# One scratch tensor for queries and keys instead of four, and another order of ScalarE, VectorE and GpSimd work, in the projection stage of a two-layer recurrent and attention kernel

## The chip, the cores and the metric

The kernel runs on one core of one Trainium2 chip. The metric is the device time of one execution in microseconds (us). A core has a tensor engine (PE, with weight loads shown as PEld), a vector engine (DVE), a scalar engine (ACT), GpSimd (POOL), and SyncE (SP), which here only issues DMA transfers. Sixteen DMA engines move the data of all transfers.

## The reference

Four sequences of 2048 tokens with 256 channels go through two layers. Each layer computes `x = x + s(xn) * silu(g(xn))` with `xn = layernorm(x)`.

```python
# layer 0: s is a WKV recurrence over time, g is a two-matrix feed-forward net
# layer 1, the part around the change:
c_q = x @ W_DQ;   Qc = c_q @ W_UQ (16 heads x 16);  Qr = rope(c_q @ W_QR) (16 heads x 8)
c_kv = x @ W_DKV; Kc = c_kv @ W_UK (16 heads x 16); Kr = rope(x @ W_KR) (8, the same for every head)
V = c_kv @ W_UV (16 heads x 16)
Q, K = concat(Qc, Qr), concat(Kc, Kr)          # 24 per head
w = softmax(where(causal, clip(Q @ K.T, -80, 80), -inf) / sqrt(24));  s = (w @ V) @ W_O
r = sigmoid(xr @ W_r.T); k = square(relu(xk @ W_k.T)); g = r * (k @ W_v.T)
# xr = mu_r * x + (1 - mu_r) * x_prev, xk the same with mu_k; x_prev is x one token earlier
```

## The kernel before, in words

The program has four stages, one after the other, each a block that all engines leave together: layer 0, the projections of layer 1 (`layer1_projections`), attention, and the output. The change is in the second stage and in what it hands to the third.

**The projection stage** goes over 16 chunks of 512 tokens (4 sequences of 4 chunks). Every engine runs its own written-out program, in order, and semaphores tie them together. Where precision matters a number is kept as two float16 halves: ACT writes the high half (`..._high`), DVE or POOL subtracts it and writes the low half (`..._low`), and PE multiplies the halves. `n` is the chunk, and work for the chunks `n + 1` and `n + 2` is threaded into the body of chunk `n`:

- **PE**: latents (`lat`), gate keys (`k_mm`), shared rotary keys (`kr_mm`), content queries (`qc_mm`), rotary queries (`qr_mm`), transposes of chunk `n + 1` (L1403, into `ps_t`, which the rotary keys also use, so they wait for DVE's two reads at L1356, `kr_parts`), then the gate receptance `r_mm` with the content keys `kc_mm` in its middle, the values, and the last gate product `kv_mm` (L1472).
- **ACT**: relu of the gate keys (L1216), `qc` high (L1219), then `xn_of(n + 1)`: `xn` high (L1162), one edge column (L1171) and four operations that write `prev`, the scaled earlier token (L1176). `kc` high (L1223) stands between the second and the third of these. Then `kr` high, the sigmoid, the values, `xk` high (L1185), `qr` high (L1240), `xr` high (L1191), the latents, `normalise(n + 2)` (four operations, L1156) and the gate's sigmoid (L1247).
- **DVE**: low halves of the latents, the two rotary key products (L1356), `qc` low, the two rotary query products, the statistics of chunk `n + 2` (`layernorm`, L1259), `kc` low (L1368), `xn` low (L1271, waits for all of `prev`), `mix` (L1280: two operations for `x_k`, two for `x_r`), `xk` low (L1285), `aggregate(n + 2)` (L1266), `qr` low (L1378), and the gate product (L1383).
- **POOL**: the rotary sums, the square, `kr` low, `xr` low (L1096), `rstd_of(n + 2)` (L1087 to L1092, four small operations whose result `normalise` waits for), and the gate (L1126).
- **SP**: the stores of the chunk, each after the semaphore of its last writer: `qc`, `kr`, `kc`, `qr`, `v` (counted in `stored`, `STORES = 5` of them per chunk) and the gate, and a load of `x` for four chunks later (none in the last four chunks). Buffers alternate between two slots. ACT waits on `stored` before it writes `qc` of a chunk two later. After the stores of chunk 12 SP issues the 20 loads of the first attention group (`load_group`: 16 for queries and keys, 4 for values). SP leaves the block only when the last `stored` count is complete, so the third stage starts then.

The scratch tensors lie in DRAM: `qc_d` and `kc_d` hold `[batch, half, 256 channels, 2048 tokens]` in float16, `qr_d` the 128 rotary query rows, `kr_d` the 8 rotary key rows. A store of `qc` is one transfer of 128 partitions with four runs of 1 KB each (512 KB). A store of `kr` is one of 8 partitions (16 KB). In attention a head has 32 partitions of its own, 24 of them used: per head and for queries and keys each, one load brings 16 content partitions (2 halves of 4 KB runs, 128 KB) and another 8 rotary partitions (64 KB).

**The attention stage** goes over 16 groups of four heads. It loads the operands of the next group while it works on this one, one transfer of SP per step.

Of the kernel before, what the change touches and what calls it, by code (L numbers as in the profile page):

```python
# [770 lines left out]
def scratch(nc):  # L771

    def dram(name, shape, dt=F32):
        return nc.dram_tensor(name, shape, dt, kind="Internal").ap()

    return {
        "x1": dram("x1_d", [TOKENS, DIM]),
        "qc": dram("qc_d", [BATCH, 2, DIM, SEQ], F16),
        "qr": dram("qr_d", [BATCH, 2, HEADS * D_R, SEQ], F16),
        "kc": dram("kc_d", [BATCH, 2, DIM, SEQ], F16),  # L780
        "kr": dram("kr_d", [BATCH, 2, D_R, SEQ], F16),
        "v": dram("v_d", [BATCH, GROUPS, P, KEYT, GH * VW]),
        "gate": dram("gate_d", [TOKENS, DIM]),
        "attn": dram("attn_d", [DIM, TOKENS]),
    }
# [65 lines left out]
STORES = 5  # L851


def layer1_projections(nc, a, d, ident, rows_out, early, scales, first):
# [6 lines left out]
    with ExitStack() as ctx:  # L861
# [130 lines left out]
        gate_v3 = d["gate"].rearrange("(n j p) c -> n p j c", j=TPC, p=P)  # L992
        LEFT, RIGHT = slice(0, 2 * LATENT), slice(2 * LATENT, 4 * LATENT)
# [30 lines left out]
        with nc.Block() as block:  # L1024
            @block.sync
            def _(sp):
# [9 lines left out]
                def store(b, c):  # L1036
# [3 lines left out]
                    sp.dma_start(d["qc"][b, :, :, t].rearrange("h (m p) t -> p (h m) t", p=P),  # L1040
                                 qc[:, s].rearrange("p h m t -> p (h m) t")).then_inc(stored[s], 16)
                    sp.wait_ge(kr_low, n + 1 + 1)
                    sp.dma_start(d["kr"][b, :, :, t].rearrange("h p t -> p h t"), kr[:, s]).then_inc(stored[s], 16)
                    sp.wait_ge(kc_low, n + 1)
                    sp.dma_start(d["kc"][b, :, :, t].rearrange("h (m p) t -> p (h m) t", p=P),
                                 kc[:, s].rearrange("p h m t -> p (h m) t")).then_inc(stored[s], 16)
                    sp.wait_ge(qr_low, n + 1)
                    sp.dma_start(d["qr"][b, :, :, t].rearrange("h p t -> p h t"), qr[:, s]).then_inc(stored[s], 16)
# [24 lines left out]
            def _(pool):  # L1073
# [32 lines left out]
                def body(b, c, left):  # L1106
# [24 lines left out]
            def _(act):  # L1131
# [27 lines left out]
                def xn_of(n, c, between=None):  # L1159
# [14 lines left out]
                    for i in (1, 0):  # L1174
# [3 lines left out]
                        if i and between:  # L1178
                            between()

                def xk_high_of(n, first=False):
# [4 lines left out]

                def xr_high_of(n, first=False):
# [13 lines left out]
                xk_high_of(0, first=True)  # L1201
                xr_high_of(0, first=True)
# [10 lines left out]
                def body(b, c, left):  # L1213
# [6 lines left out]

                    def keys_high():
                        act.wait_ge(kc_mm, n + 1)
                        nc.scalar.activation(kc[:, s, 0], ps_c[:], ACT.Copy, scale=k_factor).then_inc(kc_high, 1)  # L1223
# [28 lines left out]
            def _(dve):  # L1252
# [15 lines left out]
                def xn_low_of(n):  # L1268

                    dve.wait_ge(prev_done, PREVS * (n + 1))  # L1270
# [3 lines left out]
                def mix(n, c, first=False):  # L1274
# [3 lines left out]
                    for i, t in ((1, x_k), (0, x_r)):  # L1278
                        for k in range(KT):
# [731 lines left out]
```

## Time and profile before

| | |
|---|---|
| time, median of 3 runs | 2110.49 us (2109.88 to 2111.5) |
| the profiled execution | 2109.88 us |
| its span, first to last instruction | 2107.9 us |
| layer 0 | 0 to about 690 us |
| projections of layer 1 | about 690 to 1028.7 us |
| attention | 1028.7 to about 2040 us |
| output | about 2040 to 2107.9 us |
| mean granted TensorE clock | 0.987 of full speed |

Times in the profile are microseconds from the first instruction. A row of the timeline gives start, duration, engine, line, operation, what is written from what is read, and in brackets how long the engine was idle before it and what released it. The stages are from the timeline. One page row gives the load over the whole span: PE busy 93%, ACT 77%, DVE 76%, POOL 27%.

### The profile page before, as it was taken

Reading aid. Unit: us, or ns where it says so; the run is one execution under the profiler, and the core shown is the slowest. Engines: PE = TensorE matmul, PEld = TensorE weight load, DVE = VectorE, ACT = ScalarE, POOL = GpSimd, SP = SyncE. Lnnn points to the kernel's source line nnn. Section 1 sums busy time; section 2 is a strip of 40 time slices with the busy share of each in tenths; the row PEclk is TensorE's granted clock in tenths of the full one; section 3 lists DMA queues with packets and bytes.
Section 4 is the critical chain, followed back from the end, with each engine's and each line's share of the span. In section 5 each row is a group of like instructions: output and inputs, shape, how many; then the busy total and the mean of one; then the engine's idle time right before and its main releaser. Section 6 shows DMA issues by size and latency. Waiting matters only on the chain. (4 is left out here: it accounts for less than half of the span.)

```text
span 2107.9 us, 54312 instructions
## 1 busy us (share of the span) xinstructions
PE 1970.0 (93%) x23334; PEld 998.0 (47%) x23334; DVE 1608.8 (76%) x2223; ACT 1628.8 (77%) x1945; POOL 576.9 (27%) x416
## 2 busy tenths in 40 slices
PE   5999999999999589999899999999999999999986
PEld 2655665565565255555433444333443333343335
DVE  7867766766764777877688888888888888888877
ACT  5545644544554677787799999999999999999972
POOL 1643554454455365666200000000000000000008
PEclk9999999999999799999999999999999999999999
DMA  3000010010011255556522222222221222221229
GB/s 104 21 21 21 21 41 21 21 41 21 21 55 37 99 180 168 189 174 136 194 66 73 70 68 59 67 70 68 72 72 55 68 69 52 61 61 45 67 86 322
DMA packets 130222, 166.29 MB, mean 79 GB/s; under 512 B 13632, under 2 KB 101696, under 8 KB 129728
## 3 DMA queue, kind: packets, MB, share of 16 engines
q1 hardware_dynamic: 127952, 160.59, 25.8%
q8 instruction: 185, 3.03, 0.6%
q10 hardware_dynamic: 2032, 2.24, 0.3%
q14 instruction: 53, 0.43, 0.1%
HBM read 91.21 MB, written 71.57 MB: 77 GB/s over the span
## 5 line engine op out<-in xcount | busy, mean ns | idle before, releaser
L1683 ACT ACTIVATE c_probs<-c_ps_b 128x1536 f32<-128x1536 f32 x544 | 857.4, 1576 | 0.0
L1795 PE MATMUL c_ps_o<-c_probs,c_v 128*32 128x256 f32 (+3 forms) x6656 | 582.5, 453 | 3.8 <-DVE c_probs L1715 0.8
L1715 DVE TENSOR_SCALAR c_probs<-c_probs 128x2048 f32<-128x2048 f32 (+2 forms) x415 | 434.1, 1056 | 69.8 <-ACT c_probs L1683 67.9
L1775 PE MATMUL c_ps_a<-c_qk 24*128 24x256 f16 (+2 forms) x2688 | 444.5, 291 | 21.9 <-ACT c_probs L1682 16.6
L1775 PE MATMUL c_ps_b<-c_qk 24*128 24x256 f16 (+2 forms) x8064 | 453.4, 294 | 0.0
L1682 ACT ACTIVATE c_probs<-c_ps_a 128x512 f32<-128x512 f32 x544 | 388.7, 715 | 3.4 <-PE c_ps_b L1775 1.8
L1775 PEld LDWEIGHTS c_ps_a<-c_qk 24*128 24x128 f16 x2688 | 206.1, 92 | 369.7 <-ACT c_probs L1683 188.3
L1942 POOL TENSOR_TENSOR d_prod<-d_prod,d_x 128x1024 f32<-128x1024 f32 x8 | 26.2, 3290 | 1025.5 <-DVE d_prod L1930 1025.5
L1795 PEld LDWEIGHTS c_ps_o<-c_probs,c_v 128*32 128x32 f32 x6656 | 161.7, 108 | 245.8 <-issue 126.6
L258 POOL TENSOR_TENSOR a_hidh<-a_hid,a_hidh 128x512 f16<-128x512 f32 x128 | 170.2, 1348 | 233.6 <-ACT a_hidh L356 229.8
L1775 PEld LDWEIGHTS c_ps_b<-c_qk 24*128 24x128 f16 x8064 | 212.3, 93 | 0.8 <-issue 0.2
L1720 DVE TENSOR_SCALAR c_probs<-c_probs 128x1536 f32<-128x1536 f32 (+2 forms) x208 | 164.6, 798 | 53.0 <-ACT c_probs L1683 50.9
L667 PE MATMUL a_ps<-a_xnh,a_w 128*128 128x512 f16 x768 | 172.0, 379 | 12.0 <-ACT a_hid L351 12.0
L667 PE MATMUL a_ps<-a_w,a_hidh 128*128 128x256 f16 x1536 | 170.3, 273 | 0.0
L1724 DVE SCALAR_TENSOR_TENSOR c_probs<-c_probs,c_caps 128x512 f32<-128x512 f32 x256 | 169.7, 684 | 0.0
L667 PEld LDWEIGHTS a_ps<-a_w,a_hidh 128*128 128x128 f16 x1536 | 150.2, 98 | 17.7 <-POOL a_hidh L258 0.2
L667 PEld LDWEIGHTS a_ps<-a_xnh,a_w 128*128 128x128 f16 x768 | 73.1, 97 | 105.0 <-ACT a_hid L351 19.9
L367 ACT ACTIVATE a_gp<-a_gp 128x1024 f32<-128x1024 f32 x16 | 16.9, 1058 | 122.3 <-DVE a_gp L531 122.3
L351 ACT ACTIVATE a_hid<-a_ps,a_b 128x512 f32<-128x512 f32 x128 | 86.1, 686 | 31.8 <-PE a_ps L667 25.7
L346 ACT ACTIVATE a_en<-a_en 128x1024 f32<-128x1024 f32 x16 | 17.0, 1060 | 114.5 <-DVE a_en L499 114.5
L492 DVE TENSOR_TENSOR_SCAN a_mx<-a_decay,a_mx,a_ps 128x512 f32<-128x512 f32 x32 | 39.2, 1268 | 84.3 <-PE a_ps L667 84.2
L531 DVE SCALAR_TENSOR_TENSOR a_gp<-a_ps,a_unscale,a_b 128x1024 f32<-128x1024 f32 x16 | 20.5, 1283 | 102.1 <-PE a_ps L667 102.1
(250 smaller groups left out, 2855.7 us busy)
## 6 DMA issues: line engine op xcount, KB each, us to landing
v_d<-b_val SPq DMA_DIRECT2D x16, 1024.0 KB
c_v<-v_d SPq DMA_DIRECT2D x64, 256.0 KB
rows<-in_x SPq DMA_DIRECT2D x16, 512.0 KB, 4.8
x_d<-rows_out SPq DMA_DIRECT2D x16, 512.0 KB, 3.2
rows<-x_d SPq DMA_DIRECT2D x16, 512.0 KB, 5.0
qc_d<-b_qc SPq DMA_DIRECT2D x16, 512.0 KB
kc_d<-b_kc SPq DMA_DIRECT2D x16, 512.0 KB
gate_d<-rows_out SPq DMA_DIRECT2D x16, 512.0 KB, 3.3
```

Of the source, the lines that this page charges most:

```text
L258: nc.gpsimd.tensor_tensor(hid_half[:, 1, m], hid[:, m % RING], hid_half[:, 0, m], ALU.subtract).then_inc(hid_low, 1)
L351: nc.scalar.activation(hid[:, m % RING, :], ps_a[:, m % 2, :], ACT.Relu, bias=b_1[:, m:m + 1], scale=hid_scale).then_inc(hid_done, 1)
L492: nc.vector.tensor_tensor_scan(mx[:, k, 1:CH + 1], decay[:, k:k + 1].to_broadcast([P, CH]), ps_b[:, k, :], mx[:, k, 0:1], ALU.add, ALU.max ...
L667: mm = nc.tensor.matmul(ps, l, r, start=(first and i == 0), stop=(last and i == len(steps) - 1))
L1682: nc.scalar.activation(probs[:, t % NPROB, PARTS[0]], ps_a[:], ACT.Exp, scale=unscale).then_inc(exp_a_done, 1)
L1683: nc.scalar.activation(probs[:, t % NPROB, PARTS[1]], ps_b[:, t % 2], ACT.Exp, scale=unscale).then_inc(exp_b_done, 1)
L1715: nc.vector.tensor_scalar(tile, tile, P_MAX, P_MIN, ALU.min, ALU.max).then_inc(clip_done, 1)
L1720: nc.vector.tensor_scalar(tile[:, :, at:end], tile[:, :, at:end], P_MAX, P_MIN, ALU.min, ALU.max)
L1724: op = nc.vector.scalar_tensor_tensor(tile[:, :, at:at + P], tile[:, :, at:at + P], P_MIN, cap, ALU.max, ALU.min)
L1775: mm = nc.tensor.matmul(into, k[rows, hk, kt * P:(kt + 1) * P], tokens[rows, hq], start=(i == 0), stop=(i == len(TERMS) - 1), tile_positio ...
L1795: mm = nc.tensor.matmul(ps_o[j * VW:(j + 1) * VW, column:column + w], v[:, kt, j * VW:(j + 1) * VW], probs[:, step % NPROB, j, at:at + w], ...
L1942: nc.gpsimd.tensor_tensor(prod[:, n % OUT], prod[:, n % OUT], x1(n % SLOTS), ALU.add).then_inc(sum_done, 1)
```

## The change

1. `qc_d`, `qr_d`, `kc_d` and `kr_d` become one tensor `qk_d[batch, head, 32 rows, q or k, half, token]`. In it the content rows 0 to 15 and the rotary rows 16 to 23 of a head lie together, and the rotary keys are written once for each of the 16 heads. A chunk has 12 stores for it instead of 4 (13 with `v`).
2. `load_group` still issues 16 loads for queries and keys, each now of 24 partitions and one half (96 KB), in place of 16 or 8 partitions and both halves.
3. ACT: `kc` high comes after all four `prev` operations; `qr` high directly after `kr` high; `xk` high and `xr` high stand together.
4. DVE: `qr` low directly after `kc` low; the statistics of `n + 2` after both; `xn` low waits only for `xn` high and for the statistics; `aggregate(n + 2)` stands between the two halves of `mix`, each operation of which waits for the `prev` that it reads.
5. POOL: `rstd_of(n + 2)` comes before `xr` low of `n + 1`.

```diff
-        "qc": dram("qc_d", [BATCH, 2, DIM, SEQ], F16),
-        "qr": dram("qr_d", [BATCH, 2, HEADS * D_R, SEQ], F16),
-        "kc": dram("kc_d", [BATCH, 2, DIM, SEQ], F16),
-        "kr": dram("kr_d", [BATCH, 2, D_R, SEQ], F16),
+        "qk": dram("qk_d", [BATCH, HEADS, VW, 2, 2, SEQ], F16),
...
-STORES = 5
+STORES = 13
...
+        content = d["qk"].rearrange("b (m e) r q h t -> b m e r q h t", m=KT)
+        rotary = d["qk"].rearrange("b e r q h t -> b r e q h t")
...
                     sp.wait_ge(qc_low, n + 1)
-                    sp.dma_start(d["qc"][b, :, :, t].rearrange("h (m p) t -> p (h m) t", p=P),
-                                 qc[:, s].rearrange("p h m t -> p (h m) t")).then_inc(stored[s], 16)
+                    for h in range(2):
+                        for m in range(KT):
+                            sp.dma_start(content[b, m, :, 0:D_H, 0, h, t], qc[:, s, h, m]).then_inc(stored[s], 16)
                     sp.wait_ge(kr_low, n + 1 + 1)
-                    sp.dma_start(d["kr"][b, :, :, t].rearrange("h p t -> p h t"), kr[:, s]).then_inc(stored[s], 16)
+                    for h in range(2):
+                        sp.dma_start(rotary[b, D_H:D_QK, :, 1, h, t],
+                                     kr[:, s, h:h + 1].to_broadcast([D_R, HEADS, CH])).then_inc(stored[s], 16)
                     sp.wait_ge(kc_low, n + 1)
...
+                    for h in range(2):
+                        for m in range(KT):
+                            sp.dma_start(content[b, m, :, 0:D_H, 1, h, t], kc[:, s, h, m]).then_inc(stored[s], 16)
                     sp.wait_ge(qr_low, n + 1)
...
+                    for h in range(2):
+                        sp.dma_start(d["qk"][b, :, D_H:D_QK, 0, h, t], qr[:, s, h]).then_inc(stored[s], 16)
...
# POOL, body
+                    if left >= 2:
+                        rstd_of(n + 2)
                     if left >= 1:
                         xr_low_of(n + 1)
-                    if left >= 2:
-                        rstd_of(n + 2)
...
# ACT, body
                     if left >= 1:
-                        xn_of(n + 1, c + 1, keys_high)
-                    else:
-                        keys_high()
+                        xn_of(n + 1, c + 1)
+                    act.wait_ge(kc_mm, n + 1)
+                    nc.scalar.activation(kc[:, s, 0], ps_c[:], ACT.Copy, scale=k_factor).then_inc(kc_high, 1)
                     act.wait_ge(kr_sum, n + 1)
                     nc.scalar.activation(kr[:, s, 0, :], k_cos[:], ACT.Copy).then_inc(kr_high, 1)
+                    act.wait_ge(qr_sum, n + 1)
+                    nc.scalar.activation(qr[:, s, 0, :], q_cos[:], ACT.Copy).then_inc(qr_high, 1)
...
                     if left >= 1:
-                        xk_high_of(n + 1)
-                    act.wait_ge(qr_sum, n + 1)
-                    nc.scalar.activation(qr[:, s, 0, :], q_cos[:], ACT.Copy).then_inc(qr_high, 1)
-                    if left >= 1:
-                        xr_high_of(n + 1)
+                        mixed_high(n + 1)
                         latents_high(n + 1)
...
# DVE
-                    dve.wait_ge(prev_done, PREVS * (n + 1))
+                    dve.wait_ge(xn_high, n + 1)
...
                         for k in range(KT):
+                            dve.wait_ge(prev_done, PREVS * n + 1 + (KT + k + 1 if i == 0 else k + 1))
                             nc.vector.scalar_tensor_tensor(t[:, k, :], ps_t[:, k, :], mix_now[:, i, k:k + 1],
                                                            prev[:, i, k, 0:CH], ALU.mult, ALU.add).then_inc(mix_done, 1)
+                        if i and between:
+                            between()
...
-                    if left >= 2:
-                        layernorm(n + 2, c + 2, b + (c + 2) // XS)
                     dve.wait_ge(kc_high, n + 1)
                     nc.vector.scalar_tensor_tensor(kc[:, s, 1], ps_c[:], factor[:, WUK:WUK + 1], kc[:, s, 0],
                                                    ALU.mult, ALU.subtract).then_inc(kc_low, 1)
+                    dve.wait_ge(qr_high, n + 1)
+                    nc.vector.tensor_tensor(qr[:, s, 1, :], q_cos[:], qr[:, s, 0, :], ALU.subtract).then_inc(qr_low, 1)
+                    if left >= 2:
+                        layernorm(n + 2, c + 2, b + (c + 2) // XS)
+                        dve.wait_ge(stats_done, TPC * (n + 2) + TPC)
                     if left >= 1:
                         xn_low_of(n + 1)
-                        mix(n + 1, c + 1)
+                        mix(n + 1, c + 1, (lambda: aggregate(n + 2)) if left >= 2 else None)
                         xk_low_of(n + 1)
-                    if left >= 2:
-                        dve.wait_ge(stats_done, TPC * (n + 2) + TPC)
-                        aggregate(n + 2)
-                    dve.wait_ge(qr_high, n + 1)
-                    nc.vector.tensor_tensor(qr[:, s, 1, :], q_cos[:], qr[:, s, 0, :], ALU.subtract).then_inc(qr_low, 1)
...
 def load_group(sp, d, into, b, g, part):
...
+        j, kind, half = part // 4, part // 2 % 2, part % 2
+        sp.dma_start(into.memory[VW * j:VW * j + D_QK, kind, half], d["qk"][b, g * GH + j, 0:D_QK, kind, half]).then_inc(into.loaded, 16)
```

## Rows read from the trace of the kernel before

**Rows 1.** Windows by stage: window, length, busy of each engine, clock, DMA share, GB/s.

```profile
690.00:1028.70 338.70, 288.39 (x1570) 173.78 (x1570) 253.34 (x430) 253.85 (x370) 193.03 (x163) 0.96 0.55 172
1028.70:2040.00 1011.30, 988.28 (x17408) 397.12 (x17408) 847.73 (x1135) 1002.82 (x1089) 0.49 (x2) 0.99 0.24 63
```

**Rows 2.** Timeline of one steady chunk, ACT, DVE and POOL.

```profile
820.94 1.00 ACT L1216 ACTIVATE b_relu<-b_ps 128x1024 f32<-128x1024 f32 x1
822.75 1.01 ACT L1162 ACTIVATE b_xnh<-b_ps 128x1024 f16<-128x1024 f32 x1
823.89 1.27 ACT L1176 ACTIVATE b_prev<-b_ps,b_mix_prev 128x512 f32<-128x512 f32 x2
825.30 1.02 ACT L1223 ACTIVATE b_kc<-b_ps 128x1024 f16<-128x1024 f32 x1
825.40 1.39 DVE L1259 BATCH_NORM_STATS2 b_stats<-rows 128x6 f32<-128x256 f32 x4
...
826.72 1.27 DVE L1368 SCALAR_TENSOR_TENSOR b_kc<-b_ps,b_factor,b_kc 128x1024 f16<-128x1024 f32 x1
827.90 1.27 DVE L1271 SCALAR_TENSOR_TENSOR b_xnh<-b_ps,b_scale,b_xnh 128x1024 f16<-128x1024 f32 x1
...
829.09 1.40 DVE L1280 SCALAR_TENSOR_TENSOR b_xk<-b_ps,b_mix_now,b_prev 128x512 f32<-128x512 f32 x2
830.41 1.40 DVE L1280 SCALAR_TENSOR_TENSOR b_xr<-b_ps,b_mix_now,b_prev 128x512 f32<-128x512 f32 x2
831.73 1.22 DVE L1285 TENSOR_TENSOR b_xkh<-b_xk,b_xkh 128x1024 f16<-128x1024 f32 x1
832.86 0.37 DVE L1266 BATCH_NORM_AGGREGATE b_mv<-b_stats 128x2 f32<-128x6 f32 x4
833.13 2.67 POOL L1096 TENSOR_TENSOR b_xrh<-b_xr,b_xrh 128x1024 f16<-128x1024 f32 x1 [3.92 <-ACT b_xrh L1191]
833.15 0.66 DVE L1378 TENSOR_TENSOR b_qr<-b_qcos,b_qr 128x512 f16<-128x512 f32 x1
833.72 1.22 DVE L1383 TENSOR_TENSOR b_gi<-b_ps,b_sigr 128x1024 f32<-128x1024 f32 x1
835.76 0.19 POOL L1087 TENSOR_TENSOR b_var<-b_mv,b_eps 128x4 f32<-128x4 f32 x1
837.52 2.07 ACT L1156 ACTIVATE b_xhat<-rows,b_shift,b_rstd 128x256 f32<-128x256 f32 x4 [2.54 <-POOL b_shift L1092]
840.44 1.00 ACT L1216 ACTIVATE b_relu<-b_ps 128x1024 f32<-128x1024 f32 x1
```

**Rows 3.** Timeline of the same chunk, PE and DVE around the transposes.

```profile
834.18 2.75 PE L1410 MATMUL b_ps<-b_xkh,b_wk 128*128 128x512 f16 x12
836.87 1.47 PE L1410 MATMUL b_ps<-b_xnh,b_wkr 128*40 128x512 f16 x6
838.45 0.74 DVE L1356 SCALAR_TENSOR_TENSOR b_kcos<-b_ps,b_factor,b_cos 8x512 f32<-8x512 f32 x1 [2.05 <-PE b_ps L1410]
839.22 0.74 DVE L1356 SCALAR_TENSOR_TENSOR b_ksin<-b_ps,b_factor,b_sin 8x512 f32<-8x512 f32 x1
840.01 1.09 PE L1403 MATMUL b_ps<-ident,b_xhat 128*128 128x128 f32 x8
```

**Rows 4.** Timeline: gate stores of chunks 12 and 15, first matmul of attention.

```profile
979.51 0.36 SPq L1053 DMA_DIRECT2D gate_d<-rows_out  x1
...
1027.82 0.36 SPq L1053 DMA_DIRECT2D gate_d<-rows_out  x1
1028.73 0.55 PE L1775 MATMUL c_ps_a<-c_qk 24*128 24x512 f16 x1 [4.55 <-PEq L1024]
```

**Rows 5.** DMA view of one chunk (801.5 to 821.0), then windows: one chunk, the group loads.

```profile
DMA packets 2938, 3.45 MB, mean 177 GB/s; under 512 B 104, under 2 KB 2424, under 8 KB 2936
...
823.50:843.00 19.50, 17.77 (x98) 10.74 (x98) 14.96 (x25) 15.31 (x23) 12.00 (x11) 1.00 0.53 176
984.00:1000.00 16.00, 14.81 (x76) 8.61 (x77) 11.46 (x18) 11.95 (x18) 8.72 (x8) 1.00 1.06 108
```

More of the change, by code:

```diff
@@ L1157, in normalise, with xn_of @@
                                              scale=rstd[:, j:j + 1]).then_inc(xhat_done, 1)
-                def xn_of(n, c, between=None):
+                def xn_of(n, c):
                     act.wait_ge(xt_done, n + 1)
@@ L1177, in xn_of, with mixed_high @@
                                                  scale=mix_prev[:, i, k:k + 1]).then_inc(prev_done, 1)
-                        if i and between:
-                            between()
-                def xk_high_of(n, first=False):
+                def mixed_high(n, first=False):
                     act.wait_ge(mix_done, 2 * KT * n + KT)
@@ L1185, in xk_high_of @@
                     nc.scalar.activation(xk_half[:, 0], x_k[:], ACT.Copy).then_inc(xk_high, 1)
-                def xr_high_of(n, first=False):
                     act.wait_ge(mix_done, 2 * KT * n + 2 * KT)
@@ L1200, in _ @@
                 ckv_factor = load("b_factor_ckv", factor[:, DKV:DKV + 1])
-                xk_high_of(0, first=True)
-                xr_high_of(0, first=True)
+                mixed_high(0, first=True)
                 normalise(1, 1)
@@ L1219, in body @@
                     nc.scalar.activation(qc[:, s, 0], ps_c[:], ACT.Copy, scale=q_factor).then_inc(qc_high, 1)
-                    def keys_high():
-                        act.wait_ge(kc_mm, n + 1)
-                        nc.scalar.activation(kc[:, s, 0], ps_c[:], ACT.Copy, scale=k_factor).then_inc(kc_high, 1)
                     if left >= 1:
-                        xn_of(n + 1, c + 1, keys_high)
-                    else:
-                        keys_high()
+                        xn_of(n + 1, c + 1)
+                    act.wait_ge(kc_mm, n + 1)
+                    nc.scalar.activation(kc[:, s, 0], ps_c[:], ACT.Copy, scale=k_factor).then_inc(kc_high, 1)
                     act.wait_ge(kr_sum, n + 1)
                     nc.scalar.activation(kr[:, s, 0, :], k_cos[:], ACT.Copy).then_inc(kr_high, 1)
+                    act.wait_ge(qr_sum, n + 1)
+                    nc.scalar.activation(qr[:, s, 0, :], q_cos[:], ACT.Copy).then_inc(qr_high, 1)
                     act.wait_ge(r_mm, n + 1)
@@ L1268, in xn_low_of, with mix @@
                 def xn_low_of(n):
-                    dve.wait_ge(prev_done, PREVS * (n + 1))
+                    dve.wait_ge(xn_high, n + 1)
                     nc.vector.scalar_tensor_tensor(xn_half[:, 1], ps_t[:], scale[:, X:X + 1], xn_half[:, 0],
                                                    ALU.mult, ALU.subtract).then_inc(xn_low, 1)
-                def mix(n, c, first=False):
+                def mix(n, c, between=None, first=False):
                     if not first:
@@ L1494, in load_group @@
     if part < 4 * GH:
-        j, name, rotary = part // 4, "qk"[part // 2 % 2], part % 2
-        head, rows = g * GH + j, slice(VW * j + (D_H if rotary else 0), VW * j + (D_QK if rotary else D_H))
-        if not rotary:
-            source = d[name + "c"][b, :, head * D_H:(head + 1) * D_H, :]
-        elif name == "q":
-            source = d["qr"][b, :, head * D_R:(head + 1) * D_R, :]
-        else:
-            source = d["kr"][b]
-        sp.dma_start((into.q if name == "q" else into.k)[rows], source.rearrange("h r t -> r h t")).then_inc(into.loaded, 16)
+        j, kind, half = part // 4, part // 2 % 2, part % 2
+        sp.dma_start(into.memory[VW * j:VW * j + D_QK, kind, half], d["qk"][b, g * GH + j, 0:D_QK, kind, half]).then_inc(into.loaded, 16)
     else:
```

3 lines of the change are left out of this document (removed).

## The prediction

> **What bounds the kernel now.** I read first the stage windows [rows 1]. Attention is held by ACT, busy 1002.8 of 1011.3 us. The change alters nothing that ACT, PE or DVE do there, only the shape of loads that SP issues a whole group ahead, with DMA busy 24%. So I give attention no gain and no loss. In the projection stage no engine is full: PE is busy 288 of 338.7 us, ACT and DVE 254 each, DMA 55%. Such a stage runs at the pace of a loop of waits through several engines.
>
> The timeline of one chunk shows it [rows 2]. The relu of one chunk starts at 820.94 and the next at 840.44: 19.50 us, and so in every steady chunk (thirteen gaps in a row from chunk 1 on, within 0.03 us). Read the loop backwards from 840.44: ACT comes from `normalise` (837.52), which stood idle 2.54 us for POOL's `b_shift`; that chain begins at 835.76, right behind `xr` low (833.13, 2.67 us); that waited 3.92 us for `xr` high, which needs the second half of `mix` (830.41), which needs the first (829.09), `xn` low (827.90), `kc` low (826.72), and DVE's statistics in front of it (825.40). POOL's 2.63 us of `xr` low thus lie on the loop, and the change takes them out of it.
>
> **The change in order of work (points 3 to 5 of the change).** With `rstd_of` first it can start as soon as `aggregate` is done. But `kc` high, until now ahead of the second pair of `prev`, goes behind it, and DVE does `kc` low, `qr` low and the statistics before `xn` low. I follow the new loop from `xn` high of one chunk (time 0) with the starts and durations of [rows 2, 3]:
>
> - ACT: `prev` begins at 1.14 (823.89 less 822.75). A pair takes 1.27 and overlaps its successor by about 0.1, so four take 2.31: `kc` high from 3.45 to 4.47. In the old order it began at 2.55.
> - DVE: `kc` low at 4.51, `qr` low 1.18 later (826.72 to 827.90) at 5.69. Its `qr` high must be there: the rotary sum was ready 5.0 after `xn` high before, so it ends at 5.67, just in time. Statistics 0.57 later (833.15 to 833.72) at 6.26; they take 1.39, and `xn` low waits for their end: 7.70. First `mix` pair 1.19 later, 8.89; `aggregate` 1.32 later, 10.21; second pair 0.29 later (832.86 to 833.15), 10.50; `xk` low 1.32 later, 11.82, ending at 13.04.
> - PE: gate keys at 13.09. Before they started 834.18, 11.43 after `xn` high, when PE itself was still occupied and `xk` low (ended 832.95) was waiting for it; now PE waits. Rotary keys 2.69 later, 15.78.
> - DVE reads those at 17.36 (1.58 later, as 836.87 to 838.45) and 18.13, ending 18.87; PE transposes from 18.92 to 20.01 (1.09); `xn` high of the next chunk at 20.05.
>
> So the new loop is 20.05 us against 19.50, though the old one is cut: `rstd` would be ready at 10.6 + 1.7 = 12.3 and ACT, after the latents and `normalise`, would reach the next `qc` high at about 19.0, which ends at 20.0, just under the loop. `xn` high runs from chunk 1 to chunk 15, 14 gaps: 14 x 0.55 = **7.7 us**. The last chunk has neither statistics nor `aggregate` in its path, and I take 0.3 us more for it. The compute part of the stage ends **8.0 us** later: the last gate store is issued at 1035.8 instead of 1027.8 [rows 4]. What was saved on POOL costs nothing and gives nothing: it was one of two loops, and the other is now longer.
>
> **The stores (point 1).** The window of one chunk shows 53% DMA share over 19.5 us for 3.42 MB: 10.3 us of work on each engine, 3.0 us per MB when all sixteen share it. The DMA view of one chunk counts 104 packets under 512 B for seven transfers: six times 16 and once 8. The one that has 8 leading rows, `kr`, uses eight engines [rows 5]. The new content stores have 8 heads as their leading dimension in DRAM; I take eight engines for them also, that is 6.0 us per MB on the busiest. Per chunk there: 2.36 MB of the rest (x, gate, qr, v) 7.1 us; content 1.05 MB 6.3 us; `kr`, now 0.26 MB instead of 16 KB, 1.6 us at least. Together 15.0 us.
>
> `kr` is read from only 8 partitions. The nearest row is the group loads, which touch 16 or 8 partitions at a time: 108 GB/s at a DMA share of 1.06, where the chunk's transfers reach 176 at 0.53 [rows 5]. The query and key part of a group, 1.57 MB in 16 transfers, takes 14.5 us if only its own bytes run at 108 GB/s, and 21.1 us if the values' 1.05 MB are slowed with it (24.2 us for all, less the 3.1 us that values need at full rate). The values went through the same window, so I take 19 us, 1.2 us per transfer. The 8-row ones carry 64 KB in that, and 0.26 MB is four of them: 4.9 us for `kr`. Between 1.6 and 4.9 I take 4.9, because it is the same 8 partitions: 18.3 us per chunk, still under 20.05. For content the other bound is its 1.05 MB at 108 GB/s, 9.7 us instead of 6.3, 21.7 in all; there DMA would be the bound. I take 6.3, since it reads all 128 partitions as the gate store does.
>
> The Trainium skill ("SBUF — State Buffer", the DMA port swizzle) says that DMA bandwidth follows the number of SBUF ports reached, about 27 GB/s each, and that 8 aligned partitions reach two. By it `kr` would take 0.26 MB at 54 GB/s, 4.9 us, and a load of 24 partitions would reach six ports and take half of what one of 16 with twice the bytes per partition takes. No row here shows a read from SBUF that is limited so.
>
> SP issues 15 transfers per chunk instead of 7, at 0.36 us when the queue is free [rows 4], 5.4 us of 20; behind a waiting store on SP stand only other transfers: the gate store, needed two chunks later, and the x load, needed two chunks later too. ACT waits on `stored` only for two chunks earlier, 30 us of slack.
>
> **Where the stores show.** The stage ends with the last of them. Before, the last gate store was issued at 1027.82 and attention started at 1028.73 [rows 4], so stores were hidden. Now: the gate store of chunk 12 comes some 6 us later than its 979.5 before [rows 4], at 985.5. Behind it stand the group loads, values 3.1 us, queries and keys between 19 (as now) and 9.6 us. I take 9.6: each transfer reaches 24 partitions with 4 KB each, where it reached 16 or 8 with 8 KB. That is 998.2. Then three chunks without x load, 18.3 - 1.6 = 16.7 us each, less the last gate store, which the wait does not count (1.6): 998.2 + 50.1 - 1.6 = 1046.7. Attention starts about 0.9 later, **1047.6**, that is 18.9 us later than 1028.7: 8.0 from the loop and **10.9 of drain**.
>
> **Sum.** The profiled execution took 2109.88 us with a span of 2107.9; it is the fastest of the three shown, 0.6 under the median. 2109.9 + 18.9 = 2128.8, say **2129 us**. PE will idle longer ahead of attention, but it idled 4.55 us there before [rows 4], with a mean clock of 0.99 over attention [rows 1]; I add nothing for it. If SP's block exit were the only cover of the drain it would cost all of the 10.9; there is no other, since every engine leaves the block together.
>
> **Rivals.**
>
> - *Stores hidden, only the loop counts.* If content stores run on all sixteen engines and `kr` costs 1.6 us, a chunk is 7.1 + 3.2 + 1.6 = 11.9 us, the queue is at 998.2 + 3 x 10.3 - 1.6 = 1027.5 or waits for its data, and the last `v`, written by ACT about 1030, lands 4 us or so later, before the gate's end. Time 2118. With eight engines but cheap `kr`: 998.2 + 3 x 13.4 - 1.6 = 1036.8, and some 2 us for data that comes late, 2120. For: most rows show full-rate stores. Against: the eight completions of `kr`. Chance 0.25.
> - *The Trainium skill's engine rule.* "DMA: Bandwidth & Descriptors", why a DMA increments its semaphore by 16, gives a transfer the largest number up to 16 that divides the slowest dimension of both sides: eight for content. That agrees with the row of `kr`. In rows: that is the 6.3 us above, part of my forecast.
> - *DMA is the bound in every chunk.* If content also goes at the rate of the group loads, 21.7 us per chunk exceed 20.05. Then 12 chunks add 1.7 each (20 us), loads 19 + 3.1, three chunks 20.1 each: stage end near 1083, time 2164. With content cheap but loads at 19: 2138. For: 108 GB/s happened. Against: a store of 128 partitions is not a load of 16. Chance 0.1 beyond 2145.
> - *Faster: the cut loop was the only one.* The place is `kc` high. If it did not have to stand behind the second `prev` pair, the new loop would be 20.05 - 1.16 = 18.9, 0.6 under the old one, 14 x 0.6 = 8.4 us less: 2101 with stores hidden. It decides once my chain is over by 0.55 us in some 15 links. For: `xn` low no longer waits for `prev`, and 2.63 us leave POOL's part. Against: both queues are in order and DVE now has `kc` low ahead of `xn` low. Chance 0.07.
> - *Nothing changes.* The chain is over by 0.3 to 0.5 us, the two loops tie, and the stores are hidden: 2108 to 2114, chance 0.05.
>
> **How the numbers follow.** A measurement here tells about 0.2%, 4.2 us, from no change. My case, loop and drain (2122 to 2145), has 0.53; only the loop (2114 to 2122) 0.25; DMA-bound 0.10. Slower 0.88, same 0.05, faster 0.07. The range from 2115 to 2150 leaves out the faster and equal cases and the far end of the DMA-bound one; the likeliest case alone would be 2122 to 2145.
>
> **What the profile of the changed kernel would show.** Relu to relu 20.05 us; `xn` high waits for the transposes, not for ACT; PE idles about 0.9 us before the gate keys (L1410, from `b_xkh`) and POOL's `rstd` starts before `xr` low. Packets under 512 B per chunk: 8 for each content and `kr` store. DMA share per chunk near 0.55 to 0.65 as a mean of engines, although eight are near full. After the last gate product PE stays idle for some 14 us until attention starts near 1048. Attention itself lasts 1011 us as before. I am wrong if relu to relu is under 19.6, if attention starts under 1038 or over 1055, or if attention's steps change.

## The result, and the profile after

The changed kernel takes 2136.53 us (median of four runs, 2135.88 to 2137.05); the kernel before, in the same comparison, 2110.99 (2109.88 to 2111.79). The ratio is 1.0124, interval 1.0108 to 1.0139: slower by 25.5 us. The profiled executions are 2138.88 and 2109.88 us, 29.0 apart; the first lies 2.35 above its median and the second 1.1 below, so 3.5 of these 29.0 us are the choice of executions (two more runs of the changed kernel, outside the four, took 2137.70 and 2138.52).

The stage windows of the changed kernel (columns as in [rows 1]):

```profile
690.00:1028.70 338.70, 276.78 (x1509) 166.60 (x1510) 253.43 (x423) 247.47 (x365) 189.36 (x163) 0.96 0.60 169
1055.00:2070.00 1015.00, 988.19 (x17408) 397.30 (x17408) 847.89 (x1135) 1002.70 (x1089) 0.50 (x2) 0.99 0.22 63
```

Attention's busy times are those of [rows 1] within 0.2 us, and from its first matmul to the end of the span it takes 1079.7 us, before 1079.2. The whole loss is ahead of it. Its first matmul moved from 1028.73 [rows 4] to 1057.49, 28.8 us.

**The loop.** The timeline of one steady chunk, ACT, DVE, POOL and PE, against [rows 2, 3]:

```profile
825.39 1.01 ACT L1215 ACTIVATE b_relu<-b_ps 128x1024 f32<-128x1024 f32 x1
...
828.72 1.02 ACT L1166 ACTIVATE b_xnh<-b_ps 128x1024 f16<-128x1024 f32 x1 [0.70 <-PE b_ps L1396]
...
829.87 2.43 ACT L1180 ACTIVATE b_prev<-b_ps,b_mix_prev 128x512 f32<-128x512 f32 x4
...
832.17 1.04 ACT L1222 ACTIVATE b_kc<-b_ps 128x1024 f16<-128x1024 f32 x1
...
833.24 1.28 DVE L1361 SCALAR_TENSOR_TENSOR b_kc<-b_ps,b_factor,b_kc 128x1024 f16<-128x1024 f32 x1 [2.59 <-ACT b_kc L1222]
...
833.76 1.15 POOL L1121 TENSOR_TENSOR b_kr<-b_kcos,b_kr 8x512 f16<-8x512 f32 x1 [1.54 <-ACT b_kr L1224]
...
834.45 1.02 DVE L1364 TENSOR_TENSOR b_qr<-b_qcos,b_qr 128x512 f16<-128x512 f32 x1
...
835.38 1.40 DVE L1251 BATCH_NORM_STATS2 b_stats<-rows 128x6 f32<-128x256 f32 x4
...
836.82 1.28 DVE L1263 SCALAR_TENSOR_TENSOR b_xnh<-b_ps,b_scale,b_xnh 128x1024 f16<-128x1024 f32 x1
838.02 1.40 DVE L1273 SCALAR_TENSOR_TENSOR b_xk<-b_ps,b_mix_now,b_prev 128x512 f32<-128x512 f32 x2
...
840.91 1.22 DVE L1280 TENSOR_TENSOR b_xkh<-b_xk,b_xkh 128x1024 f16<-128x1024 f32 x1
...
841.31 0.88 POOL L1096 TENSOR_TENSOR b_shift<-b_shift,b_rstd 128x4 f32<-128x4 f32 x1
...
842.23 2.75 PE L1403 MATMUL b_ps<-b_xkh,b_wk 128*128 128x512 f16 x12 [1.23 <-issue]
...
845.86 1.01 ACT L1215 ACTIVATE b_relu<-b_ps 128x1024 f32<-128x1024 f32 x1
...
849.18 1.02 ACT L1166 ACTIVATE b_xnh<-b_ps 128x1024 f16<-128x1024 f32 x1 [0.70 <-PE b_ps L1396]
```

Relu to relu is 20.47 us, against 19.50. The order of the links is that of the prediction: `xn` high waits for the transposes, and PE stands idle 1.23 us for `xk` low (the profile names no releaser there; `xk` low ends at 842.13, and PE begins at 842.23). DVE stands idle 2.59 us for `kc` high before `kc` low, and from there to the end of `xk` low it has next to no gap. One link is longer than taken: `qr` low takes 1.02 us (median over 16 chunks 1.017), where it took 0.66 in [rows 2], and it begins while POOL's `kr` low is running, which ends at 834.91.

**The stores.** The DMA view of the chunk from 827.96 to 848.43. The first row is the busy share in 40 slices of 0.51 us, the second the rate in each:

```profile
DMA  0299987995555523444444445344554699999993
GB/s 32 86 332 300 270 202 208 328 324 190 192 192 192 188 80 68 48 46 48 46 48 48 48 48 44 22 54 134 174 184 134 206 258 308 392 390 388 408 380 140
DMA packets 3228, 3.68 MB, mean 180 GB/s; under 512 B 160, under 2 KB 2720, under 8 KB 3227
```

The small packets are 160: with 16 for each of the x load, gate and `v` and two for `qr`, that is 80, the eight content stores and two `kr` stores share the other 80, 8 each. While content stores run alone the rate is near 190 GB/s (188 to 192 in five slices); while `kr` runs it is 46 to 48 GB/s, at a DMA share of 0.44; where the stores of `qr` and `v` run, with 16 small packets each, it is 380 to 408 GB/s.

**The drain.** SP's queue from the gate store of chunk 12 to the end of the stage (a duration here is time to issue, and is long when the queue is full):

```profile
991.69 0.39 SPq L1057 DMA_DIRECT2D gate_d<-rows_out  x1
992.20 6.94 SPq L1489 DMA_DIRECT2D c_qk<-qk_d  x16
999.18 1.77 SPq L1493 DMA_DIRECT2D c_v<-v_d  x4
...
1017.72 0.61 SPq L1054 DMA_DIRECT2D v_d<-b_val  x1
...
1034.42 0.61 SPq L1054 DMA_DIRECT2D v_d<-b_val  x1
...
1041.55 1.34 SPq L1044 DMA_DIRECT2D qk_d<-b_kr  x2
1042.94 6.99 SPq L1049 DMA_DIRECT2D qk_d<-b_kc  x4
1049.97 1.23 SPq L1052 DMA_DIRECT2D qk_d<-b_qr  x2
1051.25 0.60 SPq L1054 DMA_DIRECT2D v_d<-b_val  x1
1051.89 0.56 SPq L1057 DMA_DIRECT2D gate_d<-rows_out  x1
```

The timeline around it, the last product of the gate and the first matmul of attention:

```profile
1042.13 1.23 DVE L1381 TENSOR_TENSOR rows_out<-b_gi,b_gs 128x1024 f32<-128x1024 f32 x1 [1.12 <-ACT b_gs L1239]
...
1057.49 0.58 PE L1761 MATMUL c_ps_a<-c_qk 24*128 24x512 f16 x1 [17.74 <-PEq L1023]
```

Compute ends at 1043.36, where before it ended at 1027.80, just ahead of the gate store of [rows 4]; its store can't be issued until 1051.89, because the thirteen other stores of the same chunk stand ahead of it on SP. Between the end of compute and attention lie 14.1 us; before there were 0.9. Windows of 4 us over the group loads ([rows 5] has one of 16 us for those of before), and one in the drain:

```profile
992.00:996.00 4.00, 4.00 (x35) 3.22 (x34) 2.38 (x3) 3.52 (x7) 3.96 (x3) 1.00 0.78 212
996.00:1000.00 4.00, 2.46 (x16) 1.95 (x14) 3.02 (x5) 3.75 (x6) 1.15 (x1) 1.00 0.70 158
1000.00:1004.00 4.00, 4.00 (x20) 2.44 (x19) 3.96 (x11) 0.82 (x1) 0.41 (x3) 1.00 1.04 156
1004.00:1008.00 4.00, 2.77 (x14) 1.12 (x13) 3.97 (x6) 3.48 (x7) 3.92 (x3) 1.00 0.96 198
...
1044.00:1048.00 4.00, 0.00 (x0) 0.00 (x0) 0.00 (x0) 0.00 (x0) 0.00 (x0) 0.50 0.46 76
```

Until 1057.4 no engine computes. The granted clock is 0.50, the 1.2 GHz level, while PE is idle; the mean over attention is 0.99 as before.

### The profile page after: what moved, and what is told of

The parts are those of the page before. It is cut to its first block and busy times, and to the rows that moved or that the text cites. A ratio compares the mean times of both kernels' runs of the same rounds, so it can differ in the third digit from the quotient of the medians.

```text
span 2137.2 us, 54455 instructions
## 1 busy us (share of the span) xinstructions
PE 1971.9 (92%) x23334; PEld 999.4 (47%) x23334; DVE 1616.5 (76%) x2223; ACT 1627.4 (76%) x1945; POOL 579.1 (27%) x416
## 5 line engine op out<-in xcount | busy, mean ns | idle before, releaser
L1701 DVE TENSOR_SCALAR c_probs<-c_probs 128x2048 f32<-128x2048 f32 (+2 forms) x415 | 433.8, 1055 | 69.6 <-ACT c_probs L1669 67.7
L667 PEld LDWEIGHTS a_ps<-a_w,a_hidh 128*128 128x128 f16 x1536 | 150.2, 98 | 17.8 <-POOL a_hidh L258 0.2
L531 DVE SCALAR_TENSOR_TENSOR a_gp<-a_ps,a_unscale,a_b 128x1024 f32<-128x1024 f32 x16 | 20.5, 1283 | 102.1 <-PE a_ps L667 102.1
```

The source lines that it names most:

```text
L667: mm = nc.tensor.matmul(ps, l, r, start=(first and i == 0), stop=(last and i == len(steps) - 1))
L1701: nc.vector.tensor_scalar(tile, tile, P_MAX, P_MIN, ALU.min, ALU.max).then_inc(clip_done, 1)
```

## Experiments

The theory: two losses, (a) a loop of 20.47 us instead of 19.50, which costs 14 gaps and sets when the last stores can begin, and (b) an in-order store queue that drains for 14 us after the last computation, because `kr` from 8 partitions runs at 48 GB/s and the content stores use eight DMA engines, as their packets suggest. Rivals: one of the two alone makes the whole difference; the loads, not the stores, are late; SP's number of issues rather than the rate of `kr`.

Ratios below are to the kernel before on the same chip; its median there was 2111.23 us for the first four runs, 2112.36 for the next four, 2111.35 for the last two. The end of compute is that of the last gate product.

**Order alone (e1).** Points 3 to 5 of the change, with the stores and loads of before.

> The kernel before with points 3 to 5 alone (the order of work), its own four scratch tensors and five stores. Theory: the loop is a matter of the order alone, so relu to relu is 20.47 us as in the changed kernel, and with the old stores nothing drains: attention starts about 0.9 us after the last gate store is issued, near 1044; time 2126. Rival: part of the 20.47 comes from the slower stores; then relu to relu falls to 20.05 and the time to 2120.

2126.85 us, ratio 1.0074 (1.0057 to 1.0090). Relu to relu 20.46, compute ends at 1042.32, attention starts at 1043.25, with 0.9 us between as before. The new order loses 15.6 us by itself, and no store shows.

**Layout alone (e2).** Points 1 and 2, with the order of before.

> The kernel before with points 1 and 2 alone (one tensor, twelve stores, loads of 24 partitions). Theory: relu to relu stays at 19.50, compute ends at 1027.8, but the queue needs 65.8 us from the gate store of chunk 12 (979.5) to the start of attention, as in the changed kernel: 1045.3, time 2127. Rival: the drain appears only because the compute order changed; then attention starts near 1030 and the time is 2112.

2127.62 us, ratio 1.0075 (1.0058 to 1.0092). Relu to relu 19.50, compute ends at 1028.1, attention starts only at 1045.87. The stores cost nothing per chunk, and leave 17.8 us between the last product and attention:

```profile
1026.88 1.22 DVE L1392 TENSOR_TENSOR rows_out<-b_gi,b_gs 128x1024 f32<-128x1024 f32 x1 [1.12 <-ACT b_gs L1251]
...
1045.87 0.58 PE L1772 MATMUL c_ps_a<-c_qk 24*128 24x512 f16 x1 [21.38 <-PEq L1023]
```

**Rotary keys in a tensor of their own (e3).** The new order and content stores, but `kr` stored once, not for every head, and read by one extra load per head.

```diff
+        "kr": dram("kr_d", [BATCH, 2, D_R, SEQ], F16),
...
-STORES = 13
+STORES = 12
...
-                    for h in range(2):
-                        sp.dma_start(rotary[b, D_H:D_QK, :, 1, h, t],
-                                     kr[:, s, h:h + 1].to_broadcast([D_R, HEADS, CH])).then_inc(stored[s], 16)
+                    sp.dma_start(d["kr"][b, :, :, t].rearrange("h p t -> p h t"), kr[:, s]).then_inc(stored[s], 16)
...
-    LOADS = 4 * GH + VPARTS
+    LOADS = 5 * GH + VPARTS
...
```

> The changed kernel with the rotary keys in a tensor of their own, 16 KB per chunk, one 8-partition load per head for them (20 query and key loads per group instead of 16). Theory: the replicated rotary keys, read from 8 partitions at 48 GB/s, cost 5.2 us of the busiest engines per chunk; without them three chunks of the drain lose 15.6 us and the drain is over before the compute: attention starts at 1045, relu to relu still 20.47, time 2124. Rival: the content stores on eight engines are what drains; then attention starts later than 1052.

2129.89 us, ratio 1.0086 (1.0070 to 1.0103), above the 2124 that was expected; attention starts at 1047.44 instead of 1045. Relu to relu is 20.46. `v` stores of the last three chunks are issued at 1016.06, 1028.09 and 1041.52, so 12.0 and 13.4 apart instead of 16.7 and 16.8: `kr` is worth 4.7 us of a chunk while the queue is the bound (in the last spacing SP also waited 2.3 us for `qc`). SP still issues 12 counted stores per chunk instead of 13, so the number of issues is not the cause. The drain falls from 14.1 to 4.7 us. That it doesn't fall to nothing is put down to the loads, again with an 8-partition transfer per head, which go through at 112 to 121 GB/s here and at 156 to 198 in the same windows of the changed kernel; no run tests this by itself:

```profile
996.00:1000.00 4.00, 2.46 (x13) 2.04 (x12) 3.60 (x7) 3.14 (x5) 1.15 (x1) 1.00 0.87 112
1000.00:1004.00 4.00, 4.00 (x19) 2.02 (x17) 4.00 (x9) 1.06 (x1) 1.02 (x3) 1.00 0.95 121
1004.00:1008.00 4.00, 2.77 (x13) 1.10 (x12) 3.81 (x5) 3.85 (x7) 3.35 (x3) 1.00 1.07 119
```

**`qr` low back behind `xk` low (e4).** Everything else as changed.

```diff
-                    dve.wait_ge(qr_high, n + 1)
-                    nc.vector.tensor_tensor(qr[:, s, 1, :], q_cos[:], qr[:, s, 0, :], ALU.subtract).then_inc(qr_low, 1)
                     if left >= 2:
...
                         xk_low_of(n + 1)
+                    dve.wait_ge(qr_high, n + 1)
+                    nc.vector.tensor_tensor(qr[:, s, 1, :], q_cos[:], qr[:, s, 0, :], ALU.subtract).then_inc(qr_low, 1)
```

> The changed kernel with qr low moved back behind xk low on VectorE, nothing else. Theory: qr low took 1.02 us in the loop instead of 0.66 because it started while GpSimd was in kr low (833.76 to 834.91), and with its slot it put 0.93 us (834.45 to 835.38) on the loop; without it relu to relu is 19.5 and the time falls by 12 x 0.95, about 11 us, to 2125, the drain being the same 65.8 us after the gate of chunk 12. Rival: another link (the gate product, the latents) takes its place and relu to relu stays above 20.

2126.30 us, ratio 1.0069 (1.0052 to 1.0086). Relu to relu 19.52; compute ends at 1028.87, and attention starts at 1043.71. One operation of DVE is worth 0.95 us per chunk, and `qr` low takes 0.68 to 0.69 us here, away from `kr` low. The drain is 14.8 us, and it is the loss that is left.

**Group loads five chunks in (e5).** The first group's loads go out after chunk 5 instead of chunk 12.

```diff
-                    if left == CPB - 1:
+                    if n == CPB + 1:
                         for s in range(2):
-                            sp.wait_ge(stored[s], 16 * STORES * CPB // 2 + 16)
+                            sp.wait_ge(stored[s], 16 * STORES * (CPB + 2) // 2 + 16)
```

> The changed kernel with the 20 loads of the first attention group issued after the stores of chunk 5 instead of chunk 12, waiting there for the stores of chunks 0 to 5. Theory: the slack of two us per chunk between the loop and the queue absorbs them, and the end drains only what is late by itself: behind kr low of chunk 15 (about 1036) stand 5.2 us of rotary keys, 2.8 of kc, 0.8 of qr and 3.1 of v, so attention starts near 1050 instead of 1057.5; time 2129. Rival: the queue's whole work counts, wherever it stands; then nothing changes, 2137.

2133.74 us, ratio 1.0103 (1.0086 to 1.0120). Attention starts at 1049.38, as expected, 8.1 us earlier than in the changed kernel (1.2 of that is where the stage itself began); the time is 4.7 us above what was expected, and its interval overlaps the changed kernel's. The last `v` store is issued at 1043.62, 1.6 us after compute ends, and 7.3 us still lie between the end of compute and attention: the loads are about half of the drain, and the stores are the rest.

**`kr` written twice (e6).** Each `kr` store also goes to rows 24 to 31, which nothing reads, 15 stores in all.

```diff
-STORES = 13
+STORES = 15
...
                     for h in range(2):
-                        sp.dma_start(rotary[b, D_H:D_QK, :, 1, h, t],
-                                     kr[:, s, h:h + 1].to_broadcast([D_R, HEADS, CH])).then_inc(stored[s], 16)
+                        for rows in (slice(D_H, D_QK), slice(D_QK, VW)):
+                            sp.dma_start(rotary[b, rows, :, 1, h, t],
+                                         kr[:, s, h:h + 1].to_broadcast([D_R, HEADS, CH])).then_inc(stored[s], 16)
```

> The changed kernel with the rotary keys also stored into the unused rows 24 to 31 of each head, so that their 8-partition stores double (15 counted stores per chunk). Theory: 5.2 us more per chunk on the busiest engines make 23.5 us, over the loop's 20.47; the queue becomes the bound, no slack is left (26 us over twelve chunks are used up) and the stage ends 16 x 5.2 - 26 = 57 us later: 2194. Rival: the stores wait on something other than the two ports of those partitions and overlap the others; then the time stays under 2155.

2193.48 us, ratio 1.0388 (1.0370 to 1.0405). Two more issues and 0.26 MB more per chunk cost 56 us over the changed kernel (1.0388 less 1.0124 of 2112). In the last chunks `v` stores are 22.1 and 22.7 apart instead of 16.7:

```profile
1058.23 0.60 SPq L1055 DMA_DIRECT2D v_d<-b_val  x1
...
1080.30 0.59 SPq L1055 DMA_DIRECT2D v_d<-b_val  x1
...
1103.02 0.60 SPq L1055 DMA_DIRECT2D v_d<-b_val  x1
```

A second `kr` adds 5.4 to 5.9 us, which is 0.26 MB at 44 to 49 GB/s, and with the x load a chunk's transfers exceed the loop's 20.47. The backlog builds up over a first gap of 21.3 and seven of 20.5, and then six gaps are 22.4 to 24.2: DMA has become the bound. The changed kernel is one `kr` short of that.

**Statistics ahead of `kc` low again (e7).** Everything else as changed.

```diff
+                    if left >= 2:
+                        layernorm(n + 2, c + 2, b + (c + 2) // XS)
                     dve.wait_ge(kc_high, n + 1)
...
                     if left >= 2:
-                        layernorm(n + 2, c + 2, b + (c + 2) // XS)
                         dve.wait_ge(stats_done, TPC * (n + 2) + TPC)
```

> The changed kernel with VectorE's statistics back ahead of kc low, where the engine idles 2.6 us, nothing else. Theory: they leave the loop, which falls by 1.44 us to 19.0; twelve chunks give 17 us and the drain after the gate of chunk 12 keeps its 65.8: time 2120, below the layout alone. Rival: kc high behind four prev operations is what makes the loop long; then relu to relu stays above 20.

2120.97 us, ratio 1.0043 (1.0027 to 1.0060). Relu to relu 19.02, under the 19.50 of the kernel before: the statistics now fill a part of the 2.6 us in which DVE waits for `kc` high. Compute ends at 1023.29, 4.5 us earlier than there. Attention starts at 1040.12 all the same, 11.4 later. With a faster loop the kernel is slower: the drain alone, here 16.8 us, does that.

**Only point 5 (e8).** The kernel before, with `rstd_of(n + 2)` ahead of `xr` low on POOL.

```diff
-                    if left >= 1:
-                        xr_low_of(n + 1)
                     if left >= 2:
                         rstd_of(n + 2)
+                    if left >= 1:
+                        xr_low_of(n + 1)
```

> The kernel before with GpSimd's rstd_of(n + 2) ahead of xr low, one swap of two calls, its own stores. Theory: the loop of 19.50 is cut at the 2.6 us of xr low and nothing takes its place until PE's own 17.77 us of work per chunk; relu to relu 17.8, compute ends 24 us earlier, near 1004, and the old stores and the slow group loads end about 1005; time 2087. Rival: another loop close to 19.5 holds, as in the changed kernel; then the gain is under 5 us.

2089.17 us, ratio 0.9889 (0.9872 to 0.9905): 23 us faster than before. Relu to relu is 17.81, compute ends at 1005.51 and attention starts at 1006.44, 0.9 later. PE is busy 17.51 us of a window of about one chunk, so here it is nearly the bound:

```profile
842.00:859.90 17.90, 17.51 (x100) 10.91 (x99) 15.14 (x26) 15.52 (x23) 11.81 (x10) 1.00 0.60 194
```

The loop's links, in the timeline of the same kernel:

```profile
843.50 0.66 DVE L1378 TENSOR_TENSOR b_qr<-b_qcos,b_qr 128x512 f16<-128x512 f32 x1
...
845.69 2.13 POOL L1096 TENSOR_TENSOR b_xrh<-b_xr,b_xrh 128x1024 f16<-128x1024 f32 x1
845.77 2.08 ACT L1156 ACTIVATE b_xhat<-rows,b_shift,b_rstd 128x256 f32<-128x256 f32 x4 [0.44 <-POOL b_shift L1092]
```

`normalise` waits 0.44 us for POOL instead of 2.54 [rows 2], and `xr` low takes 2.13 instead of 2.67.

**`kr` low behind `rstd_of` (e9).** In the changed kernel, so that POOL leaves `qr` low alone.

```diff
-                    pool.wait_ge(kr_high, n + 1)
-                    nc.gpsimd.tensor_tensor(kr[:, s, 1, :], k_cos[:], kr[:, s, 0, :], ALU.subtract).then_inc(kr_low, 1)
                     if left >= 2:
                         rstd_of(n + 2)
+                    pool.wait_ge(kr_high, n + 1)
+                    nc.gpsimd.tensor_tensor(kr[:, s, 1, :], k_cos[:], kr[:, s, 0, :], ALU.subtract).then_inc(kr_low, 1)
```

> The changed kernel with GpSimd's kr low moved behind rstd_of(n + 2), so that it no longer runs while VectorE starts qr low. Theory: qr low took 1.02 us instead of 0.66 because the two engines ran at once, and the 0.4 us are the difference between the 20.05 predicted for the loop and the 20.47 measured; relu to relu falls to 20.1, twelve chunks give 4.5 us, the drain may take some back because the rotary keys are stored later: time 2132 to 2135. Rival: qr low takes 1.02 us by itself in this order, and relu to relu stays at 20.47.

`qr` low takes 0.68 us and relu to relu is 20.13, as expected; compute ends at 1040.00, 3.4 us earlier. But the time is 2141.98 us, ratio 1.0142 (1.0125 to 1.0159), no better than the changed kernel's 1.0124, where 2132 to 2135 us was expected, and attention starts at 1059.95, 2.5 later. The queue of SP suggests why:

```profile
981.38 0.66 SPq L1044 DMA_DIRECT2D qk_d<-b_kr  x2
982.08 6.68 SPq L1049 DMA_DIRECT2D qk_d<-b_kc  x4
988.80 1.32 SPq L1052 DMA_DIRECT2D qk_d<-b_qr  x2
990.17 0.59 SPq L1054 DMA_DIRECT2D v_d<-b_val  x1
990.80 0.54 SPq L1057 DMA_DIRECT2D gate_d<-rows_out  x1
991.47 9.86 SPq L1489 DMA_DIRECT2D c_qk<-qk_d  x16
```

`kr` now becomes ready late (it is issued at 981.38, in the changed kernel at 978.20, although compute is ahead here); `kc`, `qr`, `v` and the gate, ready or not, stand behind it. SP no longer waits for the gate's data but goes straight from `v` to the gate store, and the queue enters the loads with a backlog (9.86 us to issue them instead of 6.94). From the gate store of chunk 12 to attention it is now 69.2 us, where the changed kernel has 65.8. This is read from the queue; no other run tests it.

**e8 with early group loads (e10).** Both edits above, on the kernel before.

> The kernel before with rstd_of ahead of xr low (as e8) and the group loads issued after chunk 5 instead of chunk 12. In e8 the last gate store was issued at 1005.53 and attention started at 1006.44, so the stage ended with compute. Theory: the queue no longer ends anything and the early loads give nothing, 2088 to 2090, the same as e8 beside the kernel before (ratio 0.989). Rival: SP's blocked time (8.5 us at 970) held compute back at the end; then 2 us more are gained.

2088.01 us, ratio 0.9884 (0.9867 to 0.9900): the same as e8, whose drain was 0.9 already.

## Why the prediction was right, and where its numbers were off

The direction, the two mechanisms and the place of each were right; the time, 2129, was 7.5 us short of the measured median. The loss was forecast as 18.9 us and measured as 25.5. Of the signs named, the small packets and attention's own steps came as said. Relu to relu (20.47 for 20.05) and the idle time before the gate keys (1.23 for 0.9) were longer, and attention's start, 1057.49, lies beyond the 1055 that was to show an error: the sizes of several terms were too small.

**The loop.** Its order of links held, and e1 shows its price alone. Of 0.97 us per gap the prediction had 0.55. The missing 0.42 is nearly all in the link "`qr` low 1.18 later, statistics 0.57 later": counted from `xn` high, the statistics begin at 6.66 instead of 6.26, and the gate keys at 13.51 instead of 13.09. The prediction took `qr` low at the 0.66 us of [rows 2], where POOL's `kr` low was not running. In the new order `kr` low and `qr` low become ready at nearly the same time. DVE's operation began 0.46 us before POOL's ended and took 0.36 longer; with `kr` low moved away it takes 0.68 and the gap is 20.13 (e9), 0.08 from the prediction's 20.05. The Trainium skill ("SBUF — State Buffer", Who interferes with whom) says that a VectorE operation with two inputs in SBUF contends with a GpSimd operation that reads SBUF, and that the order of issue decides which of the two is blocked. The trace of the changed kernel agrees either way round: `qr` low, the second of the two, was slowed, and POOL's last operation for `rstd` (L1096), which began 0.40 us after `xk` low, took 0.88 us, where it took 0.20 before, and ended 0.06 us after `xk` low. In [rows 2] `xr` low on POOL beside `qr` low took 2.67 us, and apart from it 2.12 to 2.14 (all 16 of the changed kernel, and all but the last in e8); there POOL had begun 0.02 us first and was the one slowed, so that pair doesn't bear out the order. So the term that was mis-sized is the duration of `qr` low in its new place.

Compute ends 15.6 us later rather than 8.0. Of the 7.6 us between them, 1.4 is the stage's later beginning (its first relu at 722.23 against 720.85; layer 0 is not changed, and the other runs begin between 720.9 and 722.4). Another 5.6 are in the 14 gaps of `xn` high, which together grew by 13.3 and not by 7.7; by e9's 0.34 per gap 4.8 of that are `qr` low. The last 0.6 is behind the last `xn` high, where 0.9 was lost and 0.3 was taken.

**The cut of POOL's loop.** "What was saved on POOL costs nothing and gives nothing" held for this change, but as a statement about the old kernel it hid the larger fact: POOL's tail was the loop, and cutting it alone gives 23 us (e8). The changed order put `kc` low, `qr` low and the statistics ahead of `xn` low on DVE and built a longer loop out of the saving. Of the 2.66 us per chunk between 17.81 and 20.47, `qr` low accounts for 0.95 (e4) and the statistics for 1.45 (e7), each measured alone in the changed kernel; no run takes both out at once. The rival named for faster did not come true, but a shorter loop was to be had: by POOL's swap alone (e8) and by the statistics (e7). The place that the rival named, `kc` high behind the second `prev` pair, was not run by itself. The 2.59 us that DVE waits for it in the changed kernel put it on the loop; what moving it would give is open.

**The stores.** Taken were 16.7 us per chunk on the busiest engines without an x load, and the `v` stores are 16.7 and 16.8 apart. The sum held better than its parts, which is partly luck: `kr` takes 5.5 to 5.7 us by the 46 to 48 GB/s of the DMA view (e6 gives 5.4 to 5.9, e3 4.7), where 4.9 was taken, and content's 1.05 MB take 5.5 at the 190 GB/s of that view, where 6.3 was taken. From its own rows the prediction's `kr` is four times 1.2 us, 4.8; 4.9 is what the port rule gives. That rule of the Trainium skill ("SBUF — State Buffer", Door 1: The DMA port swizzle) comes to 54 GB/s for 8 aligned partitions; measured are 46 to 48, so the trace agrees in kind and lies 11 to 15% lower. The rival "stores hidden" falls with e2, and "DMA is the bound in every chunk" with e1 and the changed kernel, whose gap is 20.46 to 20.47 with the old stores and with the new. (That rival's own sum, 985.5 + 20 + 22.1 + 60.3 - 1.6, is 1086, not 1083, which changes no chance.) The trace agrees with the Trainium skill's engine rule, which the prediction gave ("DMA: Bandwidth & Descriptors", Why a DMA increments its semaphore by 16 and not by 1): each content store has 8 small packets, and runs at about half the rate of the stores with 16.

**The drain.** Attention was expected at 1047.6 and started at 1057.49. From the gate store of chunk 12 the prediction had 62.1 us (985.5 to 1047.6), measured are 65.8. Two terms are short. The prediction put the loads right at 985.5 and left out the transfer of that gate store itself, which goes ahead of them: 1.6 us. And the loads are longer than taken: windows of 4 us from 992 to 1008 show 212, 158, 156 and 198 GB/s, mean 181, at which gate, queries, keys and values (3.14 MB) take 17.3 us; less 1.6 and 3.1 for gate and values that is an estimate of 12.6 for queries and keys, where 9.6 was taken: 3.0 us. By it the 24-partition loads are faster than the 19 us taken for the old ones, but not twice as fast. The two make 4.6 us, of which 3.7 show; 0.9 went the other way and is unplaced. Together: 1.4 (beginning), 4.8 (the loop's excess up to chunk 12: its gate store came 12.2 later instead of 6, less 1.4) and 3.7 (from that gate store on) are 9.9, which leads from 1047.6 to 1057.5.

**Why the two parts don't add up.** Order alone moves attention by 14.5 us, layout alone by 17.1, both by 28.8. With the new layout attention comes 65.6 to 67.1 us after the gate store of chunk 12, whatever the loop does after it (e2 66.0, e4 65.6, changed 65.8, e7 67.1; only e9, with its backlog, has 69.2). So only what the loop loses before chunk 12 is added to the drain; the last three chunks' loss is paid once. The medians show the same: 15.6 (e1) and 16.4 (e2) would add up to 32.0, and the changed kernel, with both, loses 25.5.

**The time.** Attention's later start, 28.8 us, is the 29.0 between the profiled executions. The prediction's sum stands against an execution of 2109.88 and came out 10.1 us under the changed kernel's own profiled time, 9.9 of them in the start of attention.

## What to carry to other kernels

Ask of every stage not only what its steady loop is but what its end waits for: stores that hide in every chunk still have to drain once, and an in-order queue makes the last one wait for everything ahead of it (e7 has the faster loop and is the slower kernel). Cut one link of a loop and measure it before anything is moved next to it; here one swap on POOL gave 1.1%, and the larger reordering around it gave that back and more. When an operation of VectorE or GpSimd is moved, look at what the other runs at that moment: a duration read from a trace holds only for its neighbours.

## What the runs showed of the hardware

- Stores from 8 partitions, 0.26 MB in two transfers, ran at 46 to 48 GB/s, and they held the queue: SP's next four issues, 0.5 MB of content from all 128 partitions, took 6.7 to 7.0 us in the steady chunks and the last one.
- VectorE and GpSimd slowed each other in turn: `qr` low went from 0.66 to 1.02 us beside `kr` low, `xr` low from 2.13 to 2.67 us beside `qr` low, and a 128x4 operation of GpSimd from 0.20 to 0.88 us beside `xk` low.
- Stores with 8 as their leading dimension in DRAM made 8 small packets each and ran near 190 GB/s, about half of the 380 to 408 of stores with 16.
- Shortening the loop by 0.34 us per chunk (e9) did not shorten the time; by the queue, the operation that was moved feeds a store that all others stand behind. Compute ended 3.4 us earlier and attention began 2.5 later.
